# First stage of a two-layer transformer kernel: evictions ahead of statistics, transposes and sums at other places in TensorE's order

## The reference, cut to what matters

```
xn = (x - mean(x)) / sqrt(var(x) + 1e-5)
k  = xn @ k_w.T + k_b                 # 2048 x 512
v  = xn @ v_w.T + v_b                 # 2048 x 512
kp = elu(k) + 1.0
kv = einsum('bhsd,bhse->bhde', kp, v) # 16 heads of 32 x 32, sums over all tokens
z  = kp.sum(over tokens)
probas = sigmoid(xn @ Wg.T)           # the router: 16 experts, the best 8 are kept
p = probas of the best 8 / their sum * 2.5
```

## Time and profile before

| what | us |
|---|---|
| median of 3 runs | 1581.12 |
| lowest and highest | 1576.73, 1583.57 |
| profiled execution, timed | 1580.7 |
| its span in the profile | 1579.0 |
| first matmul of the next stage | 146.79 |

### The profile page before, as it was taken

The page is one execution under the profiler, slowest core; times in us unless marked ns, Lnnn a source line. Parts: engine busy times, 40 slices in busy tenths (PEclk is TensorE's granted clock), DMA queues, the critical chain, the costliest instruction groups (busy, mean ns, idle before and its releaser), DMA issues. The chain is left out here.

```text
span 1579.0 us, 23584 instructions
## 1 busy us (share of the span) xinstructions
PE 1489.7 (94%) x7013; PEld 1071.0 (68%) x7013; DVE 1034.5 (66%) x2829; ACT 759.9 (48%) x1295; POOL 508.8 (32%) x723
## 2 busy tenths in 40 slices
PE   6999999999999999999998999999999988999998
PEld 4778788888766887788754545555555545787776
DVE  5553666666566658877766876666667864668582
ACT  5623665565575424433334545555555543125561
POOL 0000677777622335222211211222222223044052
PEclk9999999999999999999969999999999998999999
DMA  5002212122100434467794404324224115845021
GB/s 181 1 1 87 75 73 110 73 90 96 41 14 14 145 97 130 137 188 206 205 270 177 114 8 118 68 59 117 48 76 117 34 37 154 284 144 183 4 104 14
DMA packets 107126, 161.55 MB, mean 102 GB/s; under 512 B 12353, under 2 KB 63697, under 8 KB 100625
## 3 DMA queue, kind: packets, MB, share of 16 engines
q1 hardware_dynamic: 101868, 153.64, 32.3%
q10 hardware_dynamic: 4516, 5.38, 1.0%
q0 software_dynamic: 640, 1.31, 0.4%
HBM read 117.44 MB, written 42.87 MB: 102 GB/s over the span
## 5 line engine op out<-in xcount | busy, mean ns | idle before, releaser
L2111 ACT ACTIVATE l_pt<-banks 128x1024 f32<-128x1024 f32 (+3 forms) x288 | 218.6, 811 | 162.1 <-PE banks L1986 160.1
L2183 DVE CUSTOM_DVE_ANT_0 stage<-banks,l_edges 128x384 f32<-128x384 f32 (+3 forms) x384 | 201.5, 542 | 100.3 <-issue 99.4
L2023 PE MATMUL banks<-l_pt,l_v 128*64 128x512 f32 (+3 forms) x1152 | 230.0, 521 | 3.2 <-POOL l_pt L2081 3.2
L724 POOL TENSOR_TENSOR ex_hl<-ex_h,ex_hh 128x512 fp32r<-128x512 f32 x128 | 165.6, 1301 | 81.0 <-ACT ex_hh L692 80.8
L2080 POOL TENSOR_TENSOR l_turn<-l_before 128x2 f32<-128x2 f32 x192 | 39.8, 207 | 411.4 <-ACT l_pt L2111 400.6
L2186 DVE TENSOR_REDUCE l_mx<-banks 128x1 f32<-128x384 f32 (+1 forms) x208 | 113.1, 544 | 49.0 <-PE banks L1964 48.2
L757 DVE SCALAR_TENSOR_TENSOR ex_rw<-banks,ex_wb 128x512 f32<-128x512 f32 x128 | 88.3, 691 | 79.1 <-PE banks L75 79.0
L2023 PEld LDWEIGHTS banks<-l_pt,l_v 128*64 128x64 f32 x1152 | 70.9, 141 | 96.6 <-issue 71.5
L692 ACT ACTIVATE ex_hh<-ex_h 128x512 fp32r<-128x512 f32 x128 | 80.9, 632 | 103.6 <-DVE ex_h L765 102.3
L73 PE MATMUL banks<-ex_xlh,ex_wh 128*128 128x512 f32 x256 | 101.6, 397 | 2.1 <-DVE ex_rw L757 2.1
L1964 PE MATMUL banks<-k,q 96*128 96x384 f32 (+3 forms) x296 | 93.5, 407 | 8.9 <-DVE l_mx L2183 3.7
(11 more groups left out here) (455 smaller groups left out, 3515.9 us busy)
## 6 DMA issues: line engine op xcount, KB each, us to landing
ex_wb<-gates_by_expert SPq DMA_DIRECT2D x16, 1024.0 KB, 4.7
l_v<-layer_v SPq DMA_DIRECT2D x8, 1024.0 KB, 17.2
layer_qk<-qkv_yh SPq DMA_DIRECT2D x30, 256.0 KB, 3.2
layer_qk<-qkv_yl SPq DMA_DIRECT2D x30, 256.0 KB, 3.6
layer_v<-qkv_vs SPq DMA_DIRECT2D x15, 512.0 KB, 4.8
ex_ws<-ew_in SPq DMA_DIRECT2D x16, 384.0 KB, 5.0
l_q<-layer_qk SPq DMA_DIRECT2D x12, 512.0 KB, 7.8
l_k<-layer_qk SPq DMA_DIRECT2D x12, 512.0 KB, 14.0
```

Source lines behind the costliest of these rows:

```text
L724: pool.tensor_tensor(hl[:, k % RING, :], h[:, k % RING, :], raw(hh[:, k % RING, :]), ALU.subtract).then_inc(hl_done, 1)
L2023: last = pe.matmul(bank[h * 2 * HD:(h + 1) * 2 * HD, (qa - b * BT) * P:(qz + 1 - b * BT) * P], v[par][:, kt, h, :], pt[:, step_part(b, j), ...
L2111: act.activation(pt[:, step_part(b, j), :, 0:width], G.banks[:, 2 * slot:2 * slot + 2, 0:width], ACT.Exp, scale=scale).then_inc(p_done, 1)
L2183: dve.tensor_tensor_reduce(cutoff[:, n % 4, 0:width], G.ps[5 + n % MB][:, 0:width], masked, 1.0, NEG, ALU.add, ALU.max, mx[:, h, m, c:c + ...
```

## The change

All of it is in `stage_keys`. No instruction of computation is added or taken away; ScalarE's table loads follow from its order, and there are two more of them.

- TensorE: values(0) comes ahead of transposes(2) and (3); then values(1), keys(2), values(2), sums_of(0), transposes(4) and (5). From step 3 on the transposes of tiles 2t and 2t+1 stand in step t (before: 2t+2 and 2t+3), behind sums_of(t-2) (before: sums_of(t-1) behind values(t)) and ahead of values(t). sums_of(14) and (15) both stand at the very end.
- VectorE: the evictions of keys(0) and values(0), the low parts of tiles 2 and 3 and the eviction of values(1) come ahead of statistics(2); the steps 0 to 2 are written out; from step 3 on its loop is what it was.
- ScalarE: features(0) ahead of root(2); root(3) and root(4) in steps 2 and 3 instead of 1 and 3; some normals of xn earlier or later.

```diff
             transposes(1)
             keys(1)
             weights.ready(pe, 1)
-            for t in range(NT):
-                if t >= 2:
+            values(0)
+            transposes(2)
+            transposes(3)
+            for t in range(1, NT):
+                if t == 1:
+                    values(1)
+                    keys(2)
+                    values(2)
+                    sums_of(0)
+                    transposes(4)
+                    transposes(5)
+                elif t == 3:
+                    keys(3)
+                    sums_of(1)
+                    transposes(6)
+                    transposes(7)
+                    values(3)
+                elif t > 3:
                     keys(t)
-                if 2 <= t < AHEAD:
-                    transposes(2 * t + 2)
-                    transposes(2 * t + 3)
-                values(t)
-                if t >= 1:
-                    sums_of(t - 1)
-                if t < 2:
-                    transposes(2 * t + 2)
-                    transposes(2 * t + 3)
+                    sums_of(t - 2)
+                    if t <= AHEAD:
+                        transposes(2 * t)
+                        transposes(2 * t + 1)
+                    values(t)
...
+            sums_of(NT - 2)
             sums_of(NT - 1)
...
-            root(2)
             for t in range(NT):
-                if t in (1, 3):
-                    root(3 + t // 2)
+                if t in (2, 3):
+                    root(t + 1)
                 if t < AHEAD:
                     high(2 * t + 2)
                     high(2 * t + 3)
+                if t == 0:
+                    features(0)
+                    root(2)
                 if t + 1 < AHEAD:
                     normal(2 * t + 4)
                 if t in (0, 2):
                     weights.high(act, 4 + t // 2, 5 + t // 2)
-                features(t)
-                if t + 1 < AHEAD:
+                if t < 2:
+                    normal(2 * t + 5)
+                if t >= 1:
+                    features(t)
+                if 2 <= t < AHEAD - 1:
                     normal(2 * t + 5)
...
+            biased_keys(0)
+            biased_values(0)
+            low(2)
+            low(3)
+            biased_values(1)
+            statistics(2)
+            scales(2)
+            biased_keys(1)
+            positive(0)
+            weights.low(dve, 4, 5)
+            biased_keys(2)
+            biased_values(2)
+            low(4)
+            low(5)
+            positive(1)
+            statistics(3)
+            scales(3)
+            low(6)
+            low(7)
+            positive(2)
+            weights.low(dve, 5, 6)
+            statistics(4)
+            for t in range(3, NT):
+                biased_keys(t)
+                if t < AHEAD:
+                    low(2 * t + 2)
+                    low(2 * t + 3)
+                biased_values(t)
+                positive(t)
+                if t == 3:
+                    scales(4)
```

More of the change, by code:

```diff
@@ L508, in _, with biased_keys @@
             scales(1)
-            statistics(2)
-            scales(2)
             dve.wait_ge(bias_in, 32)
-            for t in range(NT):
+            def biased_keys(t):
                 dve.wait_ge(k_mm, t + 1)
@@ L516, in _, with biased_values @@
                 dve.tensor_tensor(kx[:, t % 2, :], pss[K[t % 2]], kbb[:, :], ALU.add).then_inc(kx_ready, 1)
-                if t < AHEAD:
-                    low(2 * t + 2)
-                    low(2 * t + 3)
+            def biased_values(t):
                 dve.wait_ge(v_mm, t + 1)
@@ L524, in _, with positive @@
                                   vbb[:, :].rearrange("p (c n) -> p c n", c=NC), ALU.add).then_inc(v_ready, 1)
+            def positive(t):
                 dve.wait_ge(e_ready, t + 1)
```

## The result

| | before | changed |
|---|---|---|
| median us | 1581.12 (5 runs) | 1595.52 (5 runs) |
| lowest and highest | 1576.73, 1583.57 | 1589.14, 1597.43 |
| profiled execution: timed, span | 1580.7, 1579.0 | 1589.1, 1587.4 |
| first matmul of the next stage | 146.79 | 155.84 |

The ratio is 1.0088, with a 95% interval of 1.0063 to 1.0112: slower, by more than I had said. So the five executions above lie on the high side of a change of about +9.4 us, 0.6%.

A forecast was written before the change was run, and what follows sets the result against it. TensorE, busy 94% of the span, was taken as the bound, with time decided by its waits. Terms -5.7, +1.2, +10.3, -0.7, -0.8 and +3.2 for clock drops gave +7.5, 1588.6 us from 1581.12; range 1582 to 1595.

The forecast's parts named there:

- Gain 1: First stage, wait before values(1): it starts 4.1 us earlier and runs 1.6 us shorter at full clock, together -5.7 us.
- Tiles 0 to 3: Start of the first stage: new small waits of 0.3, 0.4 and 0.5 us at sums_of(0), sums_of(1), logits(1), together +1.2.
- The four waits: values(4) to (7) wait for evictions behind low parts: 3.1 us once and 2.4 three times, together +10.3 us.
- Gains 2 and 3: Shorter wait at values(10) behind gates, -0.7 us; last gw transposes ahead of sums_of(14) at stage end, -0.8 us.
- The clock: TensorE's new waits in the first stage: half of four drop the clock, two drops of 1.6 us, +3.2.
- rival (b): First stage: three or all four waits drop the clock, +9.1 to +10.7 us, 1590.2 to 1591.8; chance 0.28.
- The sum: All first-stage terms, +4.3 us, with two clock drops of +3.2: +7.5 us, giving 1588.6 from the median.
- a sign of being right: The next stage's first matmul comes 7 to 8 us later than 146.79, nearly all of it gone by 90 us.
- ScalarE's table loads: Two more loads in tiles 0 to 3, 1.28 us each; at the longer price sums_of(1), values(4) wait 1.4 longer each.
- (e): Later stages start some us later and meet clock changes at other moments: 3 us allowed either way.
- within 0.5%: Whole kernel: time differs from no change by at most about 7.9 us; chance 0.50, against 0.46 slower and 0.04 faster.

The follow-up runs named there:

- e11_trace: The changed kernel unaltered, one more execution traced: 1593.2 us, next stage starting at 157.81.
- e4_shift: Kernel before plus 45 unused matmuls at the end of the first stage, so later stages start later: median 1592.84 us, ratio 1.0073.
- e13_trace_before: The kernel before, unaltered, one more execution traced: 1575.9 us.

## Why the prediction was wrong

The measured median, 1595.52, lies 0.5 us above the range of 1582 to 1595. By steps:

- **Gain 1**: held. Transposes at 24.75 and values(1) at 25.87 with the full clock; less the 0.8 by which this execution was late, 4.0 us earlier than before, where I had 4.1, and no drop.
- **Tiles 0 to 3**: waits of 0.2, 0.4 and 0.3 instead of 0.3, 0.4 and 0.5. The schedule as a whole was 0.7 short by values(4) (57.90 less 0.8 is 57.1, I had 56.4; my terms from 49.5 on add up to 6.7, so 56.2). Part of it is that a sum followed by transposes takes 0.9, not 0.81 (65.08 to 65.97), and one that had to wait takes 1.0 (42.44 to 43.44). These tenths are about what the stage cost beyond the forecast.
- **The four waits**: held. Recorded as 2.9 and three times 2.17 behind the end of the transposes, which with the 0.24 of overlap is 3.1 and 2.4, to a tenth what was laid out: 9.4 + 4 x 0.24 = 10.4 against +10.3.
- **Gains 2 and 3**: held, 0.8 each; the wait at the gates is gone, and the one at the end is 0.55 instead of 1.44.
- **The clock**: two drops of 1.6 were forecast and two came, in five of six traces; that it was half of the four was a guess between two rows, and so partly luck. The sixth had three. The comparison in rival (b) with a kernel whose clock fell at every wait left out how long its waits were; no trace here has a drop at all four. The first drop did follow the longest wait. I had no ground to say which of the 2.17 us waits would bring the other: it is the second of these three, values(6), in all six traces, and values(5) besides in the sixth.
- **The sum**: +7.5 forecast for the stage, +7.9 to +8.3 measured in five traces (less the first rise of the clock), +11.0 in the sixth, whose first values were not late (157.81 less 146.79). As recorded, with the late first values, it is 9.1 in the first trace, above the 7 to 8 that I had named as a sign of being right.
- **ScalarE's table loads**: values and sums do not wait 1.4 longer; the load of features(2) lasts 1.28 and the exp starts 0.01 behind it, so the price of load and drain did not show.

The step that failed is (e), the allowance of 3 us either way for the later stages and for what differs between executions; the mechanism of the first stage was right. I took the 3 us from three runs that differ by 6.8. Of the +14.4 between the two medians, the traced execution shows +9.1 up to the next stage and nothing behind it (1431.6 against 1432.2 us); that execution, 1589.1, is inside the range. The other four of the five are 5.6 to 8.3 us longer than it. Forty-nine executions of the kernel before differ by up to 11.5, and twenty of the changed one by up to 12.1, so a median of five of the changed kernel strays by some 4 us; a third clock drop, which I had as a rival with 0.28, is one more source. The sum was 2.2 us below what all executions show: 1588.6 against 1590.8. I had "within 0.5%" at 0.50 and slower at 0.46; it is slower, by 0.6% over all executions. With the sum at 0.47%, just under the bound, a microsecond or two of small terms on the same side decided it.

What stays open: why the first five executions (1594.7 to 1597.4 in four of them) lie above 13 of the 15 later ones. None of these four left a trace. A third drop and a low clock later, as in e11_trace at 1593.2, would do it, but that is argued, not shown. The traces may also not stand for the other executions: in nine runs with several executions (the first and eight experiments) the traced one was shorter than the mean of its fellows in eight, by 3.6 us on average over the nine. In e4_shift, which has none of the four new waits, it was shorter by 6.7, nearly as much as in the first run (7.0). So the longer executions need not come from the new waits, and what the traces say of the number of drops holds for the traced executions only.

## What to carry to other kernels

When work is moved on one engine, look at what stands ahead of its consumer on the *other* engine: here the transposes came one step later on TensorE, while VectorE kept their low parts ahead of an eviction that was ready, and TensorE waited for it four times. Put evictions that free a buffer ahead of work that depends on what the waiting engine has only just issued; one line moved turned +0.6% into -0.25%. And allow for a clock drop when TensorE waits: here waits of 2.17 to 2.9 us cost about 1.6 us above their length in some places (once 2.9) and nothing more in others. Filling the wait with useless matmuls shows how much of the cost is the clock.

## What the runs showed of the hardware

- The same wait can keep the clock or drop it: 2.17 us of standing still dropped it in one place (values(6)) in six of six traces, in another (values(5)) in one of six and in the third (values(7)) in none; waits of 1.96 to 1.98 us at the first transpose of the scores dropped it in three of six traces of the same kernel. A wait of 2.85 to 2.88 dropped it in all six, and one of 3.83 or 3.84 in all three traces of the old first stage (before, e13_trace_before, e4_shift).
- A drop costs about 1.6 us where the engine is then busy (a product takes 4.4 or 4.5 us instead of 2.8), the price of the one of 3.84; in e11_trace one lasted for at least 5.6 us and cost 1.3 us more.
- Nine useless matmuls in each of the four waits cost nothing that shows (values(5) 3.21 us behind the start of its transposes with and without them), and no drop came: 3.2 us saved in one trace.
